# Unpacking 4-bit weights ahead of or behind the transpose, in a gated-attention and MLP block

## The reference

```python
def dequant_nvfp4(W_packed, scales, block=BLOCK_SIZE):
    low = W_packed & 15
    high = W_packed >> 4 & 15
    idx = jnp.stack([low, high], axis=-1).reshape(N, -1)
    vals = NVFP4_LUT[idx]
    vals = vals.reshape(N, K // block, block) * scales[:, :, None]
    return vals.reshape(N, K)
...
x = x + jnp.tanh(g_xattn[0]) * xattn(_layernorm(x), ctx_2048, desc_router, W_q, b_q, itok)
# ffn(h): Wg, Wu are [2048, 256], Wd is [256, 2048]
gate = jnp.einsum('th,nh->tn', xt, Wg)
up = jnp.einsum('th,nh->tn', xt, Wu)
gelu = jnp.tanh(0.7978845608028654 * (gate + 0.044715 * gate ** 3)) * gate * 0.5 + gate * 0.5
out = jnp.einsum('tn,hn->th', gelu * up, Wd)
x = x + jnp.tanh(g_ffn[0]) * ffn(_layernorm(x))
```

## Time and profile before

| | us |
|---|---|
| median of three runs | 334.01 |
| lowest, highest | 332.62, 334.28 |
| the profiled execution | 334.1 |
| its span, from the first to the last instruction | 332.3 |

### The profile page before, as it was taken

The page is one execution under the profiler, slowest core; times in us unless marked ns, Lnnn a source line. Parts: engine busy times, 40 slices in busy tenths (PEclk is TensorE's granted clock), DMA queues, the critical chain, the costliest instruction groups (busy, mean ns, idle before and its releaser), DMA issues.

```text
span 332.3 us, 4521 instructions
## 1 busy us (share of the span) xinstructions
PE 316.5 (95%) x1596; PEld 258.3 (78%) x1596; DVE 221.7 (67%) x458; ACT 157.8 (47%) x291; POOL 121.7 (37%) x118
## 2 busy tenths in 40 slices
PE   6977989999999999999999999999999999999996
PEld 5645778788767788788787887788778888888885
DVE  4786889997968458577585657658584544454545
ACT  2253746576545454355434454354355354434342
POOL 5333464566443223343232333233332233323331
PEclk9599999999999999999999999999999999999999
DMA  8950240000000000000000000000000000000001
GB/s 185 285 134 0 85 136 3 0 3 0 1 2 0 0 2 0 0 1 3 0 30 3 32 0 2 0 0 3 1 32 0 34 0 2 0 32 3 32 0 65
DMA packets 10838, 9.21 MB, mean 28 GB/s; under 512 B 3328, under 2 KB 8768, under 8 KB 10816
## 3 DMA queue, kind: packets, MB, share of 16 engines
q1 hardware_dynamic: 8144, 8.33, 8.6%
q10 hardware_dynamic: 2576, 0.59, 0.9%
q0 software_dynamic: 96, 0.01, 0.0%
HBM read 6.82 MB, written 2.10 MB: 27 GB/s over the span
## 4 chain that ended last, share of the span: by engine, by line
PE 74%; DVE 14%; ACT 5%; issue 3%; DMA 2%; POOL 1%; SPq 1%; DVEq 0%; ACTq 0%; POOLq 0%
PE ring_ps L1095 45%; PE acc_ps L1129 14%; PE acc_ps L1143 7%; DVE act L807 2%; DMA x_sb<-in_x_dram 2%; DVE act L813 2%; PE att_ps L1007 2%; DVE w_lo L786 1%; ACT act L549 1%; PE att_ps L1051 1%; ACT normed L528 1%; PE ring_ps L1087 1%; DVE w_lo L791 1%; PE att_ps L1059 1%; PE att_ps L1175 1%
## 5 line engine op out<-in xcount | busy, mean ns | idle before, releaser
L419 POOL TENSOR_TENSOR act_lo<-act,act_hi 128x512 fp32r<-128x512 f32 x63 | 81.7, 1297 | 153.3 <-ACT act_hi L560 153.3
L1095 PE MATMUL ring_ps<-xt_hi,w_hi 128*128 128x512 f32 (+1 forms) x262 | 105.7, 403 | 3.6 <-DVE w_lo L791 2.0
L1095 PE MATMUL ring_ps<-xt_lo,w_hi 128*128 128x512 f32 (+1 forms) x262 | 101.2, 386 | 0.0
L1095 PE MATMUL ring_ps<-xt_hi,w_lo 128*128 128x512 f32 (+1 forms) x262 | 101.0, 385 | 0.0
L549 ACT ACTIVATE act<-ring_ps 128x512 f32<-128x512 f32 x64 | 38.3, 598 | 106.3 <-PE ring_ps L1095 104.6
L807 DVE SCALAR_TENSOR_TENSOR act<-act,ring_ps 128x512 f32<-128x512 f32 x64 | 43.9, 686 | 60.3 <-ACT act L549 60.0
L813 DVE SCALAR_TENSOR_TENSOR act<-act,ring_ps 128x512 f32<-128x512 f32 x64 | 43.8, 685 | 26.9 <-ACT act L553 26.0
L1095 PEld LDWEIGHTS ring_ps<-xt_hi,w_hi 128*128 128x128 f32 x262 | 49.3, 188 | 15.3 <-issue 4.3
L1095 PEld LDWEIGHTS ring_ps<-xt_lo,w_hi 128*128 128x128 f32 x262 | 49.2, 188 | 10.5
L1095 PEld LDWEIGHTS ring_ps<-xt_hi,w_lo 128*128 128x128 f32 x262 | 49.4, 189 | 8.0
L553 ACT ACTIVATE act<-act 128x512 f32<-128x512 f32 x64 | 40.4, 633 | 22.0 <-DVE act L807 22.0
(11 more groups left out here) (110 smaller groups left out, 312.4 us busy)
## 6 DMA issues: line engine op xcount, KB each, us to landing
out_dram<-x_sb SPq DMA_DIRECT2D x8, 256.0 KB, 2.0
x_sb<-in_x_dram SPq DMA_DIRECT2D x1, 1024.0 KB, 7.6
packed<-L_ffn_gate_W_packed_dram SPq DMA_DIRECT2D x3, 256.0 KB, 2.9
packed<-n_L_ffn_up_W_packed_dram SPq DMA_DIRECT2D x3, 256.0 KB, 3.0
packed<-L_ffn_down_W_packed_dram SPq DMA_DIRECT2D x6, 128.0 KB, 4.0
ctx_sb<-in_ctx_dram SPq DMA_DIRECT2D x2, 384.0 KB, 7.8
x_sb<-in_x_dram SPq DMA_DIRECT2D x2, 256.0 KB, 4.4
x_sb<-in_x_dram SPq DMA_DIRECT2D x1, 512.0 KB, 6.3
```

Of the source, the lines that this page charges most:

```text
L419: pool.tensor_tensor(act_lo[:, s % RING, :], act[:, s % RING, :], act_hi[:, s % RING, :].bitcast(F32), ALU.subtract).then_inc(inter_lo, 1)
L1095: i = pe.matmul(into[:, tok], wt[:, n, w], xt[:, c % 2, k, tok], start=first, stop=(k, j) == last)
```

## The change

Instead of the finished natural-order weights, PE now turns the bytes as they come.

- SP loads the int32 words one byte further on (`WORDS`, `PACK`), so that the low 16 bits of a word position hold zero and the code byte. Words that lie ahead of each row are cleared by two POOL memsets, and SP waits for them. PE transposes these 16-bit units as bf16 with a bf16 identity (`turn_bytes`), six transposes a pair, into half a bank; ACT's `compact` takes every second byte out of PSUM. `unpack` is as before, but its codes lie transposed, input features on the partitions.
- A scale now varies along both dimensions: by block over the partitions, by weight row over the columns. The scales are loaded in natural order (`scales_nat`), turned by three fp32 transposes (`turn_scales`), split by ACT into a bf16 high part and by DVE into an f32 remainder (`split_scales`), and SP copies, for each pair, eight partitions' rows to 128 partitions, each row 16 times: two DMAs of 1536 B a partition for the rows and two of 768 B for down (`spread_scales`). `spread` has two buffers; from pair 2 on SP waits for the last use of the buffer's last content.
- POOL makes the high part of the rows (`rows_high`, codes times high scales, one instruction of 512 elements a unit) and both parts of down (`down_parts`, two instructions a pair). DVE makes the rows' low parts (`rows_low`, codes times low scales, both in SBUF). The tiles, their evacuations and `w_nat` are gone.
- `ring_ps` has a plain rotation. Byte turns lie in `ring_ps` bank 3 from pair 3 on, behind up(n) in even steps; PE waits there for `inter_done` of step n - 1, and the next up waits for the compaction.
- The first two sequences are normalised on ACT (`find_shift` on DVE) instead of DVE, and the prologue's order on PE, ACT, DVE and SP is another one: turn_x(1) before score(0), warming matmuls 14, 4, 16 and 6 instead of 14 and 8, up(1) in two halves like the others.

The core of the diff:

```diff
+        def turned_in(n):
+            return [n // 2 + 2] if n % 2 == 0 and 2 <= n and n // 2 + 2 < PAIRS else []
+        def rows_made_in(n):
+            return [(n + 3) // 2] if n % 2 == 1 and (n + 3) // 2 < PAIRS else []
+        def down_made_in(n):
+            return [n // 2 + 1] if n % 2 == 0 and 2 <= n and n // 2 + 1 < PAIRS else []
...
+            def spread_scales(r):
+                if r >= 2:
+                    sp.wait_ge(hi_made, 4 * (r - 1))
+                    sp.wait_ge(lo_made, 2 * (r - 1))
+                for v in range(2):
+                    u = 2 * r + v
+                    sp.dma_start(spread[:, r % 2, v * ROW_W:(v + 1) * ROW_W],
+                                 scales_rows[u * NB:(u + 1) * NB, :].unsqueeze(1).to_broadcast([NB, P // NB, ROW_W])
+                                 ).then_inc(rows_spread[r], 16)
+                for a in range(KT):
+                    row, at = (a * PAIRS + r) * NB, 2 * ROW_W + a * DOWN_W
+                    sp.dma_start(spread[:, r % 2, at:at + DOWN_W],
+                                 scales_down[row:row + NB, :].unsqueeze(1).to_broadcast([NB, P // NB, DOWN_W])
+                                 ).then_inc(down_spread[r], 16)
...
+            sp.wait_ge(scales_split, 2)
+            spread_scales(0)
+            for m in range(2):
+                load_rows(2, m)
+            load_down(2)
+            spread_scales(1)
             load_x(CB, 2 * CB, x_next_loaded)
             load_ctx(CB, BATCH, ctx_rest_loaded)
             for i in (3, 4):
-                sp.wait_ge(compacted, 2 * (i - 2))
+                sp.wait_ge(bytes_turned, 2 * (i - 2))
...
+                for r in range(2 * i - 4, 2 * i - 2):
+                    spread_scales(r)
+            for r in (6, 7):
+                spread_scales(r)
             load_x(2 * CB, BATCH, x_rest_loaded)
...
+            def rows_high(u):
+                pool.wait_ge(unpacked, u // 2 + 1)
+                pool.wait_ge(rows_spread[u // 2], 16 * 2)
+                pool.tensor_tensor(rows_place(u, 0), rows_codes(u), rows_scales(u, 0), ALU.mult).then_inc(hi_made, 1)
+            def down_parts(r):
+                pool.wait_ge(down_spread[r], 16 * KT)
+                for part in range(2):
+                    pool.tensor_tensor(down_place(r, part), down_codes(r), down_scales_of(r, part),
+                                       ALU.mult).then_inc(hi_made, 1)
...
             def rows_low(u):
-                dve.wait_ge(rows_hi, u + 1)
-                dve.scalar_tensor_tensor(w_lo[:, u, 0:GU], bank_of("tile", tile_of(u)), FP4_SHIFT,
-                                         w_hi[:, u, 0:GU].bitcast(F32), ALU.mult, ALU.subtract).then_inc(rows_lo, 1)
+                dve.wait_ge(unpacked, u // 2 + 1)
+                dve.wait_ge(rows_spread[u // 2], 16 * 2)
+                dve.tensor_tensor(rows_place(u, 1), rows_codes(u), rows_scales(u, 1), ALU.mult).then_inc(lo_made, 1)
...
+            def turn_bytes(r):
+                if r == 0:
+                    pe.wait_ge(ident_b_made, 1)
+                for i, (r0, _) in enumerate(SECTIONS):
+                    if r == r0:
+                        pe.wait_ge(packed_loaded[i], 16 * 4)
+                if r == 1:
+                    pe.wait_ge(scales_split, 2)
+                elif r == 2:
+                    pe.wait_ge(xt_lo_ready, 1)
+                elif r > 2:
+                    pe.wait_ge(inter_done, 2 * r - 4)
+                words = packed[:, r // 2 % 2, r % 2, :]
+                for o in range(SEGS):
+                    v, m = divmod(o, 2)
+                    at = WORDS[m] + v * P if o < 4 else WORDS[2 + m]
+                    units = words[:, at:at + P].bitcast(BF16).rearrange("p (j two) -> p j two", two=2)[:, :, 0]
+                    i = pe.transpose(bytes_bank(r)[:, o * P:(o + 1) * P], units, ident_b[:, :])
+                i.then_inc(bytes_turned, 1)
...
             update_stats(0)
             update_variance(0)
-            normalise(0)
+            find_where(1)
+            find_shift(0)
             weigh(1)
             rows_low(0)
+            rows_low(1)
             ln2_low(0)
...
             update_stats(1)
             update_variance(1)
-            normalise(1)
+            find_shift(1)
+            for stage in range(3):
+                unpack(1, stage)
             ln2_low(1)
             rows_low(2)
+            rows_low(3)
             cubic(0)
             cubic(1)
             gated_of(0)
```

## The result

The changed kernel takes 353.13 us (median of 4 runs, 350.97 to 354.64) where the kernel before takes 334.06: a ratio of 1.058, 95% interval 1.051 to 1.064. It is slower by 19 us; I had forecast 326.8 us, in a range of 322.5 to 345.0. The profiled execution has a span of 351.5 us, against 332.3 before.

What follows compares the result with a forecast made beforehand. TensorE was taken to bound the kernel, DVE close behind; after the change DVE's path would set steps 3 to 15. 334.1 - 2.0 (up to gate(2)) - 2.0 (step 2) - 3.3 (steps 3 to 15) = 326.8 us, range 322.5 to 345.

Steps and rivals of the forecast that it cites:

- steps 3 to 15: Conversion stretch of chunk 0, 68.8 us before: forecast 65.5 us, -3.3, ends 63.0 and 70.5.
- step 2: gate(2) to gate(3), 7.93 us before: forecast 5.8 us, -2.0, ends -2.5 and 0.
- the spreads: SP's scale-spreading DMAs: up to about 5 us a pair, hidden by three steps (15 us), or 6 us in the prologue.
- DVE's path: DVE in steps 3 to 15: 60.4 us busy plus gaps makes 65.5 us, passing TensorE's 63.0.
- rival (c): Spreads are the bound, 12.3 us a pair: 343.6 us, up to 354; chance 0.36. Signs: late landings, idle DVE and POOL.
- My 343 us: Whole-kernel estimate for slow spreads from the skill's 27 GB/s a port: 54 GB/s, 10.9 us a pair.
- the 343.6: Whole-kernel time if spreads run 12.3 us a pair: pair 7's rows land no sooner than 107.8, gate(16) at 122, +9.5.
- SP's queue: Loads behind the spreads: packed loads and 1 MB of x for the last chunks, both taken as covered.
- DVE's low parts: Ten rows' low parts in steps 3 to 15 wait for POOL 0.6 us each (0.35 to 1.1): +6.0 us.
- The clock: Prologue, 9.0 to 15.6 us: granted clock left at 0.50; a fall in the prologue's new gaps named as a possible miss.
- TensorE's floor: Steps 3 to 15: 68.8 less 7.6 for tile turns plus 1.8 for byte turns, 63.0 us.
- Up to gate(2): Prologue, 35.75 us before: gate(2) at 33.7, -2.0, ends -3 and +1.

Runs made afterwards that it cites:

- the table in HBM: Changed kernel, but every spread reads 128 contiguous rows of packed weights in HBM instead of 8 SBUF partitions (wrong scales): 343.48 us.
- the PSUM operand: Changed kernel, spreads reading 128 HBM rows, both low parts between cubic and gated, their scales from gate(s)'s PSUM bank (wrong scales): 333.3 us; SBUF-operand control 345.1.
- the low parts on ACT: Changed kernel, spreads reading 128 HBM rows; from pair 2 ACT copies codes without scales in place of DVE's low parts (wrong result): 328.42 us.
- 128 source partitions: Changed kernel, but each spread reads all 128 SBUF partitions once instead of 8 partitions 16 times each (wrong scales): 341.19 us.

## Why the prediction was wrong, point by point

The forecast's term for steps 3 to 15 was 65.5 us. From gate(3) to gate(16) the changed kernel takes 83.5, the one with the table in HBM 79.7, with the PSUM operand 69.9, and with the low parts on ACT 65.1. With the table in HBM gate(2) is 2.5 us later than forecast, step 2 is 0.3 shorter and steps 3 to 15 are 14.2 longer; the slow spreads add 9.7 us to that kernel's time. So two steps failed: the spreads taken as hidden, and DVE's path in steps 3 to 15 taken as one sum, the dearer of the two.

**The spreads**, taken at "up to about 5 us a pair", hidden. This step failed first in time, and it was named as rival (c) with 0.36. Its bound from the earlier trace rows, 48 GB/s, was right (47 to 64 measured), and I took the other end because only writing into few partitions had been seen. The Trainium skill's port rule ("SBUF — State Buffer", "Door 1: The DMA port swizzle"), from which I had estimated 54 GB/s, lies between them, near enough that the trace agrees, though the stretch at 64 is above it. My 343 us by that estimate was not made like the 343.6 beside it: it has the 10 us of other loads in it, which the 343.6 leaves out, and without them it would be no loss at all. Two signs of (c) came: landings 8.9 and 10.6 us behind their issue (25.93 to 34.8, 38.82 to 49.4), and idle time of DVE and POOL that ends at a spread. But the 3 to 8 us were to come at rows_low(2), where DVE idles only 1.9 us (2.7 at rows_low(0)); the 7.56 come at rows_low(4). And the arithmetic did not hold. I had priced the stream of eight pairs, with the loss at pair 7. In fact no spread is waited for from pair 3 on; two steps take 12.9 us there on average, and a pair's spreads 10. The 10 us are lost at the first three pairs, where the forecast had 6 us of cover. That (c)'s price of 9.5 us is close to them is luck.

**SP's queue.** I had the packed loads and the x of the last chunks behind the spreads, "covered", and passed over the x for chunk 1. Spreads hold SP while they are issued, 6.9 us for two, and PE waits 4.35 us for x; moving it gave 3.4 us.

**DVE's low parts**, 0.6 us of waiting each in steps 3 to 15, between 0.35 and 1.1. Measured: 1.17 us on average for 0.68, so 0.5: well sized. POOL's high part is 1.10 us by itself where I had 1.06, but it waits as well (1.39 on average), which the sum left out. What failed is the next line, DVE's path as one sum over 13 steps. 60.4 us of work in 65.5 looks like slack. But the work isn't spread evenly: in step 5 two low parts, the search for the picked sets and the weights fall together, PE's queue has the probabilities at its front, and every such heap is a stall; steps 6 to 7, 8 to 9 and 12 to 13 take 10.7, 9.3 and 9.7 us in the changed kernel beside others of 4.08. Priced by runs: the exclusion 10.0 us of the stretch, DVE's own load 4.9 us (333.3 to 328.4). That the heaps are what makes them so dear is a reading of the timelines; no run spreads the same work evenly.

**The clock.** "I leave it so" for the prologue, and nothing for the rest. PEclk fell to 0.90 over steps 3 to 15. From gate(3) to gate(16) TensorE was busy for 67.3 us, and for 60.8 with the low parts on ACT, where the same 290 matmul records ran at a clock of 1.00: 6.5 us that I had not counted. I had written down that it might fall in the prologue's gaps, and gave it no price.

**TensorE's floor**, 63.0 us for steps 3 to 15, was a little high. With the low parts on ACT the stretch takes 65.1 us, of which PE waits 3.9: 61.2 of its own. The 63.0 was made from 68.8 us, in which TensorE idles 1.5. A byte turn costs 0.32 us to the next matmul (45.29 to 45.61); my 0.45 had 0.09 for that matmul in it.

**Step 2**, -2.0 us: with fast spreads and 128 source partitions gate(2) to gate(3) is 5.66 us where I had 5.8, from 7.93. Right.

**Up to gate(2)**, -2.0 us: wrong even with fast spreads. In the kernel with 128 source partitions (DVE, PE):

```profile
31.29 2.20 DVE L778 TENSOR_TENSOR w_lo<-code_bits,spread 128x512 fp32r<-128x512 fp8e5 x2
33.40 0.68 DVE L790 SCALAR_TENSOR_TENSOR act<-act,ring_ps 128x512 f32<-128x512 f32 x1
...
35.94 0.47 PE L1080 MATMUL ring_ps<-xt_hi,w_hi 128*128 128x512 f32 x1 [0.94 <-DVE act L796]
```

gate(2) comes at 35.94 for 35.75. The two low parts ahead of cubic(0) take 2.20 us, near the bad end that I had named. And xt_lo of sequence 1, which I had ready at 28.9, is ready at 31.37, 0.6 us later than before; the probabilities ahead of it reach PE at 23.02 for 21.98.

## What to carry to other kernels

Ask of every new DMA how many partitions it reads as well as writes, and what stands behind it in the queue that issues it. When a change gives two engines work that excludes each other, it isn't enough to add the waits to a sum of busy times: lay them out step by step against the positions in the in-order queues of those who wait, since here one overloaded step stalled TensorE and took its clock along. And ask whether an operand can lie in PSUM: there the exclusion of those DVE instructions by POOL was gone. What it costs to bring the right scales there was not measured.

## What the runs showed of the hardware that I had not expected

- A DMA out of 8 SBUF partitions, each row 16 times, runs at 47 to 64 GB/s, with the DMA share of the table at 0.45, and holds the issuing queue for 6.9 us (two of 96 KB). The same shape out of HBM runs at 163 GB/s at a share of 0.56 and is issued in 1.2 us for two; behind x, ctx and packed weights the issue of two took 4.3 us. 128 SBUF partitions as the source run at 322 GB/s at 1.12 and land 192 KB in 2.3 us.
- One PSUM operand in place of one from SBUF changes the same DVE instruction from 1186 to 1797 ns to 680 to 683 ns beside a busy POOL.
- The clock between 9.0 and 15.6 us was 0.50 before the change, 1.00 after it, and 0.54 with 128 source partitions. I didn't look for what sets that; it stays open, and gate(2) did not follow it.
- PEclk over 51 to 113 us was 0.89 in the changed kernel, 0.97 with the PSUM operand and 1.00 with the low parts on ACT. Some of what taking work from DVE gains is therefore gained as clock.
